# A perceiver block on one core: the work between attention and experts in another order, and parts of it moved to GpSimd and into the expert stage

## The reference

```
x = x + cross_attention(layernorm(x), ctx, ctx, mask)      # 16 heads of 16, biases
x = x + causal_self_attention(layernorm(x))                # 16 heads of 16, rotary angles
x = x + moe(layernorm(x))
```

```
logits = x @ router_w                                      # (8, 128, 8)
dispatch, combine = gating_top2(logits, C=32)              # (8, 128, 8, 32) each
expert_inputs = einsum('GSEC,GSM->EGCM', dispatch, x)
hidden = gelu(expert_inputs @ w0) * (expert_inputs @ w1)   # 1368 wide
expert_outputs = hidden @ wo
out = einsum('EGCM,GSEC->GSM', expert_outputs, combine)
```

## Time and profile before

| | us |
|---|---|
| median of 3 runs | 539.72 |
| the 3 runs | 535.71, 539.72, 540.93 |
| profiled execution | 542.8 |
| its span, first to last instruction | 541.0 |
| mean granted TensorE clock | 0.946 |

### The profile page before, as it was taken

The page is one execution under the profiler, slowest core; times in us unless marked ns, Lnnn a source line. Parts: engine busy times, 40 slices in busy tenths (PEclk is TensorE's granted clock), DMA queues, the critical chain, the costliest instruction groups (busy, mean ns, idle before and its releaser), DMA issues.

```text
span 541.0 us, 18283 instructions
## 1 busy us (share of the span) xinstructions
PE 495.8 (92%) x6637; PEld 456.4 (84%) x6637; DVE 394.0 (73%) x1007; ACT 324.6 (60%) x839; POOL 256.6 (47%) x343
## 2 busy tenths in 40 slices
PE   1898999998999999999996578999999999999996
PEld 0777888788888898888875467999999999999995
DVE  2545555676676667677687867789999999999963
ACT  1456776665677577577652336666666676666640
POOL 4134345335434353643452011666666766667640
PEclk9979999999999999999997665899999999999998
DMA  6523111111111111110009000364565646556202
GB/s 171 187 74 88 26 42 40 43 42 23 42 22 39 39 28 31 39 39 2 3 5 310 3 1 1 118 197 154 162 231 176 188 145 197 171 160 217 80 1 78
DMA packets 58126, 48.92 MB, mean 90 GB/s; under 512 B 20942, under 2 KB 49744, under 8 KB 58064
## 3 DMA queue, kind: packets, MB, share of 16 engines
q1 hardware_dynamic: 58064, 48.09, 30.3%
HBM read 46.86 MB, written 1.08 MB: 89 GB/s over the span
## 4 chain that ended last, share of the span: by engine, by line
PE 81%; issue 6%; ACT 4%; DVE 3%; DMA 3%; SPq 1%; POOL 1%; ACTq 0%; DVEq 0%; POOLq 0%
PE bank L225 20%; PE bank L227 18%; PE bank L226 18%; PE bank L638 5%; PE bank L606 3%; PE bank L659 3%; PE bank L563 2%; ACT Pr L1094 2%; PE bank L1024 2%; DMA w_raw<-in_L_xattn_Wk 2%; PE bank L913 2%; PE bank L795 1%; DMA last_prob<-Pr 1%; PE bank L766 1%; PE bank L755 1%
## 5 line engine op out<-in xcount | busy, mean ns | idle before, releaser
L225 PE MATMUL bank<-XT_lo,W_hi 128*128 128x256 f32 (+1 forms) x352 | 100.5, 286 | 1.4 <-ACT XT_lo L1282 1.4
L226 PE MATMUL bank<-XT_hi,W_lo 128*128 128x256 f32 (+1 forms) x352 | 100.1, 284 | 0.0
L227 PE MATMUL bank<-XT_hi,W_hi 128*128 128x256 f32 (+1 forms) x352 | 99.8, 284 | 0.0
L2275 POOL TENSOR_TENSOR W_lo<-raw,W_hi 128x256 fp32r<-128x256 f32 (+1 forms) x88 | 87.7, 996 | 7.0
L2190 POOL TENSOR_TENSOR Pr<-Pr,rinv 128x1028 f32<-128x1028 f32 (+2 forms) x32 | 60.5, 1890 | 49.6 <-DVE rinv L1441 48.9
L1094 ACT ACTIVATE Pr<-Sc,nmax 128x257 f32<-128x257 f32 x128 | 63.8, 501 | 22.2 <-DVE nmax L1430 19.5
L1430 DVE CUSTOM_DVE_ANT_0 Sc<-bank,mask_add 128x257 f32<-128x257 f32 x128 | 47.0, 423 | 40.0 <-PE bank L606 17.3
L1922 DVE TENSOR_TENSOR W_lo<-raw,W_hi 128x512 fp32r<-128x512 f32 (+1 forms) x88 | 69.4, 789 | 4.6 <-ACT W_hi L1261 1.1
L2116 DVE TENSOR_TENSOR hid_lo<-hid,hid_hi 128x256 fp32r<-128x256 f32 (+1 forms) x88 | 71.6, 814 | 1.5 <-ACT hid_hi L1337 1.5
L2273 POOL CAST W_hi<-raw 128x256 fp32r<-128x256 f32 (+1 forms) x88 | 39.9, 453 | 63.3 <-PE bank L227 37.4
L225 PEld LDWEIGHTS bank<-XT_lo,W_hi 128*128 128x128 f32 (+1 forms) x352 | 66.5, 189 | 1.7 <-issue 1.7
(11 more groups left out here) (243 smaller groups left out, 1329.9 us busy)
## 6 DMA issues: line engine op xcount, KB each, us to landing
raw<-in_L_ffn_w_kernel SPq DMA_DIRECT2D x32, 512.0 KB, 4.7
ctx_raw<-in_ctx SPq DMA_DIRECT2D x32, 256.0 KB, 2.9
raw<-in_L_ffn_wo_kernel SPq DMA_DIRECT2D x16, 512.0 KB, 5.8
raw<-in_L_ffn_w_kernel SPq DMA_DIRECT2D x16, 344.0 KB
last_prob<-Pr SPq DMA_DIRECT2D x128, 1.0 KB, 1.8
raw<-in_L_ffn_wo_kernel SPq DMA_DIRECT2D x8, 256.0 KB
x_sb<-in_x SPq DMA_DIRECT2D x4, 256.0 KB, 6.0
VL_all<-vl_rows SPq DMA_DIRECT2D x8, 128.0 KB
```

Of the source, the lines that this page charges most:

```text
L225: pe.matmul(dst, a_hi, b_lo, start=first, stop=False)
L226: pe.matmul(dst, a_lo, b_hi, start=False, stop=False)
L227: return pe.matmul(dst, a_hi, b_hi, start=False, stop=last)
L2275: po.tensor_tensor(W2_lo[0:w, m % RW, :], raw2[0:w, t, :], f(W2_hi[0:w, m % RW, :]), ALU.subtract)\
```

## The change

The calls of the tail stand in another order on PE, ACT, DVE and POOL. On DVE `weigh` and `disperse` are gone. POOL makes the dispatch matrices of tiles 0 to 4 (`disperse`: two comparisons and one sum, from `past`, which `place_early` now computes on DVE in two more steps) and the weights of all tiles (`weigh`); the weights of tiles 4 to 7 are made in steps 1 to 4 of the expert stage, each ahead of that step's split of the down weights. DVE makes the dispatch matrices of tiles 5, 6 and 7 (`disperse_late`), each in two operations. `disp` has four buffers in place of two. All four turnings of the weights lie in steps 2, 4, 6 and 8 of the expert stage. The last tile's `XT_lo` is copied by DVE. At the end the eight tiles are merged in the order 0, 2, 4, 6, 1, 3, 5, 7, each in a bank given by a table; first products of four tiles stand ahead of or right behind the last `down`, and the sum goes to `x_sb` itself, so that `fin` with its four buffers is gone.

```
-    past = sb("past", [P, 2], scope=early)
-    disp = sb("disp", [P, 2, E * CAP], F32R, early)
+    DR = 4
+    past = sb("past", [P, 2, TT], scope=early)
+    disp = sb("disp", [P, DR, E * CAP], F32R, early)
...
+    TURN_AT = [2, 4, 6, 8]
+    MERGE = [0, 2, 4, 6, 1, 3, 5, 7]
+    MERGE_BANK = [6, 1, 4, 2, 5, 0, 3, 7]
...
@@ tensor
+        def combine(j, k):
+
+            t = MERGE[j]
+            last = pe.matmul(bk[MERGE_BANK[j]][:, 0:D], CT[:, t, k, :], Y[:, t, k, :], start=k == 0, stop=k == 1)
+            if k == 1:
+                last.then_inc(sm["comb_made"], 1)
...
         up(*place(1))
-        turn_weights_of(TT // 2 - 1)
         for m in range(ALL):
             up(*place(m + 2))
+            if m in TURN_AT:
+                turn_weights_of(TURN_AT.index(m))
+            if m == ALL - 1:
+                pe.wait_ge(sm["ct_read"], TT // 2)
+                pe.wait_ge(sm["y_read_act"], E)
+                pe.wait_ge(sm["y_read_dve"], E)
+                combine(0, 0)
+                pe.wait_ge(sm["h_done"], done(*place(ALL - 3)))
             down(*place(m))
-        for t in range(TT):
-            for k in range(2):
-                last = pe.matmul(bk[t][:, 0:D], CT[:, t, k, :], Y[:, t, k, :], start=k == 0, stop=k == 1)
-            last.then_inc(sm["comb_made"], 1)
+        combine(1, 0)
+        pe.wait_ge(sm["h_done"], done(*place(ALL - 2)))
+        combine(2, 0)
+        combine(3, 0)
+        pe.wait_ge(sm["y_part_act"], 1)
+        combine(0, 1)
+        pe.wait_ge(sm["y_part_dve"], 1)
+        combine(1, 1)
+        combine(2, 1)
+        combine(3, 1)
+        pe.wait_ge(sm["h_done"], done(*place(ALL - 1)))
+        pe.wait_ge(sm["y_read_act"], E + 1)
         pe.wait_ge(sm["y_read_dve"], E + 1)
+        for j in range(4, TT):
+            combine(j, 0)
+            combine(j, 1)
...
@@ scalar, behind hid_hi(m)
-            if m == 0:
-                keep_weights_of(TT // 2 - 1)
+            if m in TURN_AT:
+                keep_weights_of(TURN_AT.index(m))
...
@@ vector
+        def disperse_late(t):
+
+            need(("reach", t))
+            if t >= DR:
+                ve.wait_ge(sm["r_x_made"], t - DR + 1)
+            mark(("disp0", t), ve.tensor_scalar(disp[:, t % DR, :], slot_no, past[:, 0, one(t)], None, ALU.is_equal))
+            need(("disp0", t))
+            ve.scalar_tensor_tensor(out=disp[:, t % DR, :], in0=slot_no, scalar=past[:, 1, one(t)],
+                                    in1=f(disp[:, t % DR, :]), op0=ALU.is_equal, op1=ALU.add).then_inc(sm["d_disp"], 1)
+
+        def keep_last_inputs():
+
+            ve.wait_ge(sm["r_x_made"], TT)
+            ve.tensor_copy(XT_lo[:, :, :, (TT - 1) * CAP:TT * CAP],
+                           inputs_of(TT - 1)[1].rearrange("p (k e c) -> p k e c", k=KH, e=E)).then_inc(sm["last_kept"], 1)
...
@@ gpsimd
+        def disperse(t):
+
+            po.wait_ge(sm["r_reach"], 1)
+            if t >= DR:
+                po.wait_ge(sm["r_x_made"], t - DR + 1)
+            if t > 0:
+                po.wait_ge(sm["r_disp"], 3 * t)
+            po.tensor_scalar(second[:, :], slot_no, past[:, 1, one(t)], None, ALU.is_equal).then_inc(sm["r_disp"], 1)
+            po.tensor_scalar(disp[:, t % DR, :], slot_no, past[:, 0, one(t)], None, ALU.is_equal).then_inc(sm["r_disp"], 1)
+            po.wait_ge(sm["r_disp"], 3 * t + 2)
+            po.tensor_tensor(disp[:, t % DR, :], f(disp[:, t % DR, :]), second[:, :], ALU.add).then_inc(sm["r_disp"], 1)
...
+            if 0 < m <= TT - EARLY + 1:
+                weigh(EARLY - 2 + m)
```

More of the change, by code:

```diff
@@ L945, in _ @@
         logits(v_)
-        positions(0, EARLY)
         turn_norm(z)
         project_self(z, False)
-        project_self(z, True)
+        positions(0, EARLY)
         turn_self_probs(y_)
         turn_qk(z)
+        scores(z)
         self_outputs(y_)
-        scores(z)
+        project_self(z, True)
         project_out(y_)
         dispatch(0)
-        dispatch(1)
-        turn_self_probs(z)
-        turn_router(y_)
-        positions(v_, y_)
-        logits(y_)
-        self_outputs(z)
-        turn_weights_of(0)
+        turn_self_probs(z)
+        positions(v_, y_)
+        self_outputs(z)
+        turn_router(y_)
+        project_out(z)
+        logits(y_)
+        dispatch(1)
         dispatch(2)
-        project_out(z)
+        turn_router(z)
+        logits(z)
+        positions(y_, z)
         dispatch(3)
-        turn_router(z)
-        positions(y_, z)
-        logits(z)
         dispatch(4)
-        turn_weights_of(1)
+        positions(z, TT)
         dispatch(v_)
-        positions(z, TT)
         dispatch(y_)
-        turn_weights_of(2)
         dispatch(z)
         pe.wait_ge(sm["r_x_kept"], TT)
+        pe.wait_ge(sm["last_kept"], 1)
         def up(half_, n):
@@ L1997, in _ @@
         turn_angles(z, 2)
-        choose(v_, 2)
+        choose(v_, 6)
         add_rotated(z)
         spread_probs(y_)
-        weigh(0, 0)
-        weigh(0, 1)
-        choose(v_, 3)
         spread_queries(z)
-        weigh(0, 2)
-        choose(v_, 4)
+        place_early(0)
+        place_early(1)
+        choose(v_, 7)
+        place_early(2)
+        place_early(3)
+        choose(v_, 8)
+        place_early(4)
+        choose(v_, 9)
+        place_early(5)
+        place_early(6)
+        place_early(7)
@@ L2007, in _ @@
+        place_early(8)
         scale_scores(z)
-        choose(v_, 5)
         max_scores(z)
-        disperse(0)
         less_max(z)
         split_self(y_)
-        weigh(1, 0)
+        sum_probs(z)
+        invert_self(z)
+        scale_probs(z)
         norm_step(y_, "c", 0)
-        choose(v_, 6)
         norm_step(y_, "c", 1)
-        weigh(1, 1)
         norm_step(y_, "c", 2)
-        choose(v_, 7)
         norm_step(y_, "c", 3)
-        sum_probs(z)
-        weigh(1, 2)
-        invert_self(z)
@@ L2024, in _ @@
-        choose(v_, 8)
-        scale_probs(z)
-        norm_step(y_, "c", 4)
-        disperse(1)
-        spread_probs(z)
-        choose(v_, 9)
-        weigh(2, 0)
-        weigh(2, 1)
-        weigh(2, 2)
-        disperse(2)
-        weigh(3, 0)
+        spread_probs(z)
+        norm_step(y_, "c", 4)
+        slots_of(v_, 0)
+        slots_of(v_, 1)
+        slots_of(v_, 2)
+        slots_of(v_, 3)
+        slots_of(v_, 4)
+        slots_of(v_, 6)
+        slots_of(v_, 7)
+        slots_of(v_, 5)
@@ L2035, in _ @@
+        split_self(z)
+        disperse_late(v_)
+        norm_step(z, "c", 0)
+        norm_step(z, "c", 1)
+        norm_step(z, "c", 2)
+        norm_step(z, "c", 3)
         read_logits(y_)
-        split_self(z)
         choose(y_, 0)
-        slots_of(v_, 0)
         choose(y_, 1)
-        slots_of(v_, 1)
+        norm_step(z, "c", 4)
         choose(y_, 2)
-        slots_of(v_, 2)
-        norm_step(z, "c", 0)
+        choose(y_, 3)
         choose(y_, 4)
-        norm_step(z, "c", 1)
-        slots_of(v_, 3)
@@ L2069, in _ @@
-        disperse(v_)
         read_logits(z)
+        choose(z, 0)
+        choose(z, 1)
+        choose(z, 2)
+        choose(z, 4)
         slots_of(y_, 0)
-        choose(z, 0)
+        choose(z, 5)
         slots_of(y_, 1)
-        choose(z, 1)
+        choose(z, 6)
         slots_of(y_, 2)
-        choose(z, 2)
         choose(z, 3)
-        choose(z, 4)
+        choose(z, 7)
         slots_of(y_, 3)
-        choose(z, 5)
         slots_of(y_, 4)
-        choose(z, 6)
-        slots_of(y_, 5)
@@ L2084, in _ @@
-        choose(z, 7)
-        weigh(y_, 0)
-        weigh(y_, 1)
-        weigh(y_, 2)
-        disperse(y_)
+        slots_of(y_, 6)
+        slots_of(y_, 7)
+        disperse_late(y_)
         slots_of(z, 0)
@@ L2097, in _ @@
         slots_of(z, 7)
-        disperse_last()
+        disperse_late(z)
+        choose(z, 8)
+        choose(z, 9)
+        keep_last_inputs()
         split(0, 1)
         split(0, 2)
+        slots_of(y_, 5)
         slots_of(z, 5)
-        weigh(z, 0)
-        weigh(z, 1)
-        weigh(z, 2)
         for m in range(ALL):
@@ L2258, in _ @@
         scale_probs(y_)
+        disperse(0)
+        disperse(1)
+        disperse(2)
+        disperse(3)
         power(y_, "c")
         keep_normed(y_)
+        disperse(4)
+        weigh(0)
+        weigh(1)
         power(z, "c")
         keep_normed(z)
+        weigh(2)
+        weigh(3)
         po.wait_ge(sm["r_x_kept"], TT)
+        po.wait_ge(sm["last_kept"], 1)
         po.sem_inc(sm["split_pool"], 1)
```

163 lines of the change are left out of this document (65 added, 98 removed).

## The result

The changed kernel takes 549.52 us in the median of four runs (547.87 to 551.36), the kernel before 538.09 in four on the same chip (535.71 to 540.93). The ratio is 1.021, with a 95% interval of 1.014 to 1.029: slower, by about 2%. I had said 536.5, with a range from 530.5 to 541.5.

The account below looks back on a forecast made before the run. PE bounds the expert stage, a chain from engine to engine the tail. Tail −4.7, turnings +1.35, ACT's wait +4.0, end stage −3.9 sum to −3.25 us: 536.5 us against the median of 539.72, range 530.5 to 541.5.

Parts of the forecast that it names:

- POOL's price: Tail and expert stage: one `disperse` or `weigh` on POOL takes 2.0 us, bounds 1.8 to 3.5.
- Nothing lost: Tail: tile 6's power, queued behind four `disperse`, is 1.7 us late, but PE needs its result only at 311.0.
- Hidden, by 1.7: Expert stage: split 4 is ready 15.2 us after the start, `down(4)` begins at 16.9, so POOL's `weigh` costs zero.
- D: Rival: POOL becomes the bound at 3.6 per `disperse`, delaying tail and expert stage; +6.5, 546.2 us; chance 0.07.
- My signs of being wrong: First expert product after 334, PE's expert-stage stalls above 6 us in sum, or POOL's comparisons above 1.0.
- (a) to (c): Tail, last tile: norm turning, scores and self outputs no longer queue behind other work; scores at 299.6, self outputs 309.1, 6.5 earlier.
- (d), (g): Tail, last tile: out projection at 312.4, 6.8 us earlier; last copy shared by two engines, first expert product 329.1, 6.7 earlier.
- (h): Tail: DVE operations that meet POOL's work from 316 to 324 run slower, costing 2.0 us, bounds 0 to 6.
- (e): Tail: a new wait, DVE idle some 3 us for `dispatch(1)`; normed tile at 319.0, 4.2 us earlier.
- Turnings: Expert stage: four transposes of the weights at 0.43 less the old 0.37 cost PE +1.35 us.
- ACT's wait: Expert stage: ACT's copy of turned weights delays the next gelu, stalling PE 1.0 per turning; +4.0 us, 3.0 to 5.4.
- End stage: Final merge: reordered products leave PE no idle time before the clock falls; −3.9 us, or −2.2 if it falls anyway.

Follow-up runs that it names:

- e6: The change with the same operations on POOL in another order, each power and the split behind it as early as its input allows; 547.69 us, ratio 1.015.
- e4: The change with the dispatch matrices of tiles 0 to 4 also made on DVE, in two operations each; 541.19 us, ratio 1.005.
- e5: The change with ACT's copy of turned weights one step later, weights of tiles 4 to 7 over steps 1 to 10, early dispatch matrices on DVE; 534.11 us.
- e3: The change with the twelve operations of the last four `weigh` spread over ten steps of the expert stage instead of four; 546.36 us, ratio 1.013.
- e1: The kernel before with nothing but the new end stage; 536.53 us, ratio 0.995.
- e8: e1 with all four turnings in the expert stage, ACT's copy one step later; tail order, weights and dispatch matrices as before; 538.79 us, ratio 0.999.

## Why the prediction was wrong

**The step that failed** is "POOL's price": "I take 2.0, near the one-input row, since a comparison reads one tile". A `disperse` costs 2.9 on average (300.24 to 311.77 for four), a `weigh` 3.4; its two operations that compare and multiply are 1.22 each, a form that I had priced like the plain comparison. The bounds I had written, 1.8 to 3.5, held both. I chose between them by the count of inputs, from a cast, which is another kind of instruction; and my own text had a warning against it, the power of one element at 0.55 us. From this one value came two zeros:
- *"Nothing lost" in the tail.* The first power was 5.6 us late instead of 1.7, the second, which I had not costed at all, 2.6. PE was idle 4.09 at the one, DVE 2.63 at the other; e6, which only moves the powers forward in POOL's list, gives 5.1 us back in the tail, and e4, which frees POOL, 6.5. The text let the loss begin at 2.4 per `disperse`, with 0.4 for each 0.1 above: 1.9 us at 2.88. Two things were missing. PE was ready at 308.76, and not at 309.85 (my 311.0, less the 1.15 between the spans): 1.1, of which 0.85 since it ran `self_outputs(z)` in 1.08 us at full clock, which I had at 1.93. And behind the last `disperse` the power and the norm still take 1.08 (311.77 to 312.85), so that the loss begins at 2.15: another 1.0. Together 4.0.
- *"Hidden, by 1.7" in the expert stage.* `weigh` and split repeat every 4.4 to 5.2 us (342.31 to 347.52, 347.52 to 352.43, 352.43 to 356.79) against the 3.5 I took. Split 4 was ready 21.0 us after the stage's start (356.85), and not 15.2. Three waits, 3.6 us; and behind the longest of them the clock fell, 1.7 us in the two stretches from 345.8 on. In e5 waits of 1.3 us are left, and the clock stays up from 340 to 360; that the wait brought the clock down is my reading, since no run changes the one without the other.

**The rival that came true is D**, at a chance of 0.07: it named the mechanism, both places and 546.2 us. It took 3.6 per `disperse`; at 2.9 it had put the balance at no change. The measured loss at 2.9 is bigger than that, for the reasons above (the second power, the loss that begins at 2.15) and the clock. So D had the mechanism right and its size partly by luck: +6.5 in its sum and +5.1 between the two profiled executions, from a price 0.7 too high and terms that it lacked. The chance was too small for the size of the bounds: between 1.8 and 3.5, with the turn at 2.9, a third lay on the wrong side. My signs of being wrong were too loose for the same reason. The first expert product came late, as the first of them says (335.81 is 336.96 in the old span, my limit 334), but PE's stalls in the expert stage sum to 5.65, below my 6, and a plain comparison took 0.92, below my 1.0.

The Trainium skill (GPSIMD Engine Reference, Engine selection) puts one-input work on POOL as roughly even with DVE. No run agrees for this form: the comparison with a number per partition took 0.35 on DVE (318.62) and 0.92 on POOL, and with a second operation 0.40 on DVE and 1.22 on POOL; the measurement decides. It was not what my number came from, but it stood beside it and agreed, where it should have been doubted with it.

**What held.** Moments are counted from the normed tile 5 in each trace, since the spans begin their tails 1.15 us apart.
- (a) to (c): scores predicted at 14.3, measured 14.65 (298.78 − 284.13); self outputs predicted 23.8, measured 23.55 in the change and 24.06 in e4.
- (d), (g): out projection predicted 27.1, measured 27.21 in e4 (309.64 − 282.43), 31.05 in the change. First expert product with (h) predicted 45.8, measured 45.22 in e4 and 45.20 in e5. In e4 the tail's −4.7 is −5.3, with `self_outputs(z)` 0.85 shorter by the clock there too, and with another order on DVE: the walk is right to about 1 us, and not to the 0.6 that these numbers show.
- (e): DVE idle 3.59 for `dispatch(1)`, predicted some 3.
- (h): did not come as told. Between 316 and 324 no DVE operation is slow, since DVE stands still for most of that time. Slow ones beside POOL lie elsewhere: 0.91 for a matrix of 0.35 (332.11), 0.65 for a step of 0.22 (328.64), 0.60 for one of 0.16 (313.59); the longest, 1.00 for 0.23 (293.54), met the scaling of tile 6, which POOL did before too. e4 and e5 reach −5.3 of the walk's −6.7, which leaves about 1.4 us for collisions if the walk is right in all else; I took 2.0.
- Turnings: +1.35 predicted, 1.0 measured.
- ACT's wait: 0.75 to 1.35 each, 4.0 in sum, predicted; 0.41, 0.69, 0.95 measured, as the first turning fell together with a wait for POOL; 0.98, 1.22, 0.39 and 0.96 where nothing else delayed PE (e3). The mechanism is right; the sum is 2.05 in the change, below my 3.0 to 5.4, and 3.55 in e3.
- End stage: −3.9 predicted, −4.5 in the change and −4.4 in e1.

In sum, the spans differ by −1.15 before the tail, +1.1, +9.5 and −4.5, which is +5.0. The medians of the runs differ by 11.4. The other 6.4 is the choice of executions: the profiled one of before lies 4.7 above its median of 538.09, that of the change 1.6 below its own. My forecast of 536.5 is 13.0 below the median. Of these 8.35 are seen in the two profiled executions (−3.25 forecast, +5.1 measured); the other 4.7 are the 3.1 that I took off, since the profiled run of before was above its median, and the 1.6 of the change.

**What stays open.** e1 shows one part of that scatter, the clock at the first expert products; why it is up in some executions and down in others no run tells apart. Each kernel has one trace, so that it is this place which differs in the other runs too is not shown. Whether the powers early and the weights spread would have saved the change with POOL's work as it is, was not run. In the expert stage e5 takes 195.14 and e8 193.52, with 1.3 us of waits for POOL in e5 and a clock in the first ten us of 0.79 against 0.70 in e8; about 1 us of that difference is not assigned. How much of DVE's slower steps is owed to POOL in the tail was not tried by itself.
